# Attention stacks of 64 rows: two heads side by side on the array, 32-row tiles for half of batch 0 only, and a new order of the work

## The reference

```python
x = x + attn(layernorm(x))     # 16 heads of 8, causal, biases on q, k, v and the output
x = x + xattn(layernorm(x), ctx, mask)   # keys and values from 77 context tokens, masked per batch
x = x + ffn(layernorm(x))      # 8 experts of 128x128, gate, top 2 of 8, weights p / sum, halved

scores = einsum('bntd,bnsd->bnts', q, k) / sqrt(D)        # D = 8
scores = where(causal, scores, -inf); attn = softmax(scores); out = einsum(attn, v)
```

## Time and profile before

| | us |
|---|---|
| median of three runs | 424.85 (424.1 to 430.12) |
| the profiled execution | 431.44 |
| its span | 429.6, mean granted clock of TensorE 0.833 |
| TensorE busy | 375.8 (87%) |
| VectorE busy | 255.5 (59%) |
| ScalarE busy | 181.2 (42%) |
| GpSimd busy | 135.1 (31%) |

### The profile page before, as it was taken

How to read it: one execution, slowest core, us unless ns; L and a number is a source line. 1 busy time by engine, 2 the same in 40 slices (tenths; PEclk the granted TensorE clock), 3 DMA queues, 4 the chain that set the end, 5 groups by cost and what they waited for, 6 DMA issues and landing times.

```text
span 429.6 us, 6790 instructions
## 1 busy us (share of the span) xinstructions
PE 375.8 (87%) x2478; PEld 193.3 (45%) x2478; DVE 255.5 (59%) x684; ACT 181.2 (42%) x345; POOL 135.1 (31%) x198
## 2 busy tenths in 40 slices
PE   8989799999987699999789889948789799999593
PEld 3553556344443254445444434315444565724350
DVE  5383645488824499736689988113876324345467
ACT  1712112355675264887560148853445422131100
POOL 3662200122254222125333542221217300005613
PEclk9985555599998699999999989987989855559878
DMA  4654560000036700024320000050000000000000
GB/s 132 147 81 65 92 93 3 1 5 4 1 69 74 83 0 4 7 40 84 58 44 2 5 29 2 2 71 4 2 5 2 24 2 0 2 0 1 27 0 24
DMA packets 19509, 13.82 MB, mean 32 GB/s; under 512 B 2684, under 2 KB 19476, under 8 KB 19476
## 3 DMA queue, kind: packets, MB, share of 16 engines
q1 hardware_dynamic: 19074, 13.04, 17.6%
q10 hardware_dynamic: 402, 0.34, 0.3%
HBM read 2.71 MB, written 1.05 MB: 9 GB/s over the span
## 4 chain that ended last, share of the span: by engine, by line
PE 54%; DVE 23%; ACT 9%; issue 6%; POOL 4%; DMA 3%; ACTq 1%; SPq 1%; DVEq 0%; POOLq 0%
DVE peaks L908 6%; PE banks L1250 6%; PE banks L1061 6%; PE banks L1234 6%; PE banks L1151 5%; PE banks L1053 4%; PE banks L1176 3%; PE banks L1201 3%; PE banks L1275 3%; PE banks L1304 3%; DVE xpeaks L921 3%; PE banks L1266 3%; PE banks L1049 2%; POOL yw L700 2%; PE banks L1082 2%
## 5 line engine op out<-in xcount | busy, mean ns | idle before, releaser
L796 ACT ACTIVATE probs<-banks 128x512 f32<-128x512 f32 x160 | 88.2, 603 | 84.0 <-PE banks L1234 76.0
L908 DVE TENSOR_REDUCE peaks<-banks 128x1 f32<-128x384 f32 (+3 forms) x132 | 76.0, 635 | 24.0 <-PE banks L1176 23.9
L689 POOL TENSOR_SCALAR_AFFINE_SELECT probs<-probs 128x512 f32<-128x512 f32 (+1 forms) x80 | 43.8, 547 | 146.8 <-ACT probs L796 146.8
L1234 PE MATMUL banks<-q_stack,k_stack 102*128 102x512 bf16 (+3 forms) x256 | 55.5, 322 | 3.6 <-ACT probs L796 1.3
L700 POOL TENSOR_TENSOR yw<-yw 128x512 f32<-128x512 f32 (+2 forms) x42 | 34.4, 818 | 63.7 <-issue 32.9
L802 ACT ACTIVATE xprobs<-banks 77x512 f32<-77x512 f32 x64 | 34.3, 604 | 31.6 <-PE banks L1266 24.7
L915 DVE TENSOR_REDUCE peaks<-banks 128x1 f32<-128x128 f32 (+2 forms) x64 | 27.7, 519 | 31.8 <-PE banks L1151 31.8
L1250 PE MATMUL banks<-probs,v_s 128*9 128x256 f32 (+3 forms) x512 | 45.7, 454 | 0.6 <-POOL probs L689 0.3
L1176 PE MATMUL banks<-k_stack,q_stack 96*128 96x512 bf16 (+2 forms) x144 | 44.2, 356 | 0.0
L1167 PE MATMUL banks<-causal,ident_b 128*128 128x128 bf16 (+2 forms) x132 | 33.6, 255 | 7.9 <-issue 6.4
L1234 PEld LDWEIGHTS banks<-q_stack,k_stack 102*128 102x128 bf16 x256 | 20.9, 102 | 42.0 <-issue 17.2
(11 more groups left out here) (168 smaller groups left out, 539.0 us busy)
## 6 DMA issues: line engine op xcount, KB each, us to landing
q_stack<-parts_q SPq DMA_DIRECT2D x24, 128.0 KB, 3.8
k_stack<-parts_k SPq DMA_DIRECT2D x48, 64.0 KB
xq_stack<-parts_x SPq DMA_DIRECT2D x18, 128.0 KB, 4.4
state<-in_x SPq DMA_DIRECT2D x4, 256.0 KB, 4.6
out<-state SPq DMA_DIRECT2D x4, 256.0 KB, 2.3
expert_w_s<-in_expert_w SPq DMA_DIRECT2D x1, 512.0 KB, 4.3
...
```

What stands on the lines that cost most here:

```text
L689: gp.affine_select(out=v, in_=v, compare_op=ALU.is_ge, fill=0.0, base=0, pattern=pattern, channel_multiplier=-1).then_inc(causal_done, 1)
L796: ac.activation(probs[:, grp % 2, u, :], bank_of(step), ACT.Exp, scale=SCALE).then_inc(taken_of(step), 1)
L908: ve.tensor_reduce(dst, bank_of(step)[:, 0:n * width].rearrange("p (h k) -> p h k", h=n), X_AXIS, ALU.max, negate=True).then_inc(taken_of( ...
L1234: last = te.matmul(bank_of(step)[:, col:col + n], k_stack[0:ROWS, b % 2, s, p, 128 * kt:128 * kt + 128], q_stack[0:ROWS, b % 2, p, 128 * k ...
```

## The change

- The stacks have 64 rows for each head (`SLOT`), the two heads of a pair in rows 0 to 63 and 64 to 127. A feature's six parts lie in a step of 8 rows, the mask of the cross attention in row 6 and the maxima, now in two parts, in rows 62 and 63. A product of scores, peaks, cross scores or cross peaks uses 64 rows. `k_stack` and `xk_stack` lose their place for the head.
- The keys are copied by six DMAs of 16 rows, as the queries. Rows that no part fills are cleared: q_stack by ScalarE, xq_stack and xk_stack by GpSimd, k_stack by VectorE.
- The mask is added with 64-row weights (`pick_slot`, `causal_slot`), in two products of 128 columns per head and bank in place of one.
- The peaks of a bank are of heads in the same 64 rows; `SCORES` joins units of the same head slot.
- Only the first half of batch 0 has its peaks in 32-row tiles; the second half uses the stacks. Batch 3's cross attention stays in 32-row tiles.
- The split of the maxima loses its last operation.
- `plan()` has other costs and another `ORDER` and `AHEAD`, and its model of TensorE has tiles, a time for changes of the tiling, and a clock. `WARM` is 0: all products of ones in waits go. Eight at the start (L1066) stay.

The diff, cut to its core:

```diff
-MAX_ROW, ROWS = 96, 102
-MASK_ROW, XMAX_ROW, XROWS = 96, 97, 103
+STEP, SLOT = 8, 64
+MASK_ROW, MAX_ROW, ROWS = 6, 62, 64
 Q_PARTS = (0, 0, 0, 1, 1, 2)
 K_PARTS = (0, 1, 2, 0, 1, 0)
-STACK_DMAS = {"q": len(Q_PARTS), "k": 2 * len(K_PARTS), "x": len(Q_PARTS)}
+STACK_DMAS = len(Q_PARTS)
...
-TILED_PEAKS, TILED_CROSS = 0, B - 1
-
-
-PEAKS = ([(0, [(p, None) for p in (2 * i, 2 * i + 1)]) for i in range(2)]
-         + [(1, [(p, None)]) for p in range(4)]
-         + [(t, [(p, s)]) for t in (2, 3) for p in range(4) for s in range(2)])
+TILED_PEAKS = ((0, 0),)
+TILED_CROSS = B - 1
+
+
+PEAKS = ([(0, s, (0, 1, 2, 3)) for s in range(2)]
+         + [(1, s, (p, p + 1)) for p in (0, 2) for s in range(2)]
+         + [(t, s, (p,)) for t in (2, 3) for p in range(4) for s in range(2)])
 
 TILE_PEAKS = (((0, 0), (1, 128)), ((2, 0),), ((3, 0),))
 
-XPEAKS = [(t, h, n) for t in range(T) for h, n in ((0, 6), (6, 5), (11, 5))]
+XPEAKS = [(s, n, min(n + 6, T * PAIRS)) for n in range(0, T * PAIRS, 6) for s in range(2)]
 
 
 SCORES = ([[(0, j, 0)] for j in range(4)]
           + [[(0, j, 3), (128, j, 1)] for j in range(4)]
-          + [[(0, j, 2), (256, j + 1, 2)] for j in (0, 2)])
+          + [[(0, j, 2), (256, j + 2, 2)] for j in (0, 1)])
...
-BANKS, WARM_BANK = 8, 7
+BANKS, CAUSAL_BANKS = 8, (6, 7)
...
-LATENCY, HOP, SWITCH, RANK, ISSUE = 0.22, 0.05, 0.0, 0.0, 0.62
-AHEAD = {'peak': 4, 'tile_peak': 3, 'xpeak': 2, 'tile_xpeak': 5, 'scores': 2, 'xscores': 5, 'tile_xscores': 5, 'expert': 5}
-
-ORDER = ('scores', 'experts', 'cross', 'scale', 'peaks', 'prepare', 'attend', 'context')
+LATENCY, HOP, SWITCH, ISSUE, LAND = 0.22, 0.05, 0.0, 1.06, 2.7
...
+WARM = 0
+DRAIN, FORCE, CHILL = 0.09, 0, 0
+BIAS = (0.0, 0.0, 0.0, 0.0, 0.0, 0.2, 0.0, 0.0)
+AHEAD = {'peak': 3, 'tile_peak': 3, 'xpeak': 2, 'tile_xpeak': 1, 'scores': 2, 'xscores': 5, 'tile_xscores': 3, 'expert': 6}
+
+ORDER = ('scores', 'cross', 'scale', 'peaks', 'prepare', 'attend', 'context', 'experts')
...
-            key = (start + SWITCH * switch + RANK * rank, rank)
+            key = (start + SWITCH * switch + BIAS[rank], rank)
             if best is None or key < best[0]:
...
-                steps.append(("warm", len(steps), idle))
-            tile = tile_of(step)
+                    steps += [("warm", len(steps), (i, bank_uses[i], count))] * WARM
...
+            size, rows = tile_of(step)
+            if switch:
+                start += DRAIN
+            mode = size
...
         q_stack = sb("q_stack", [128, 2, PAIRS, S], BF16)
-        k_stack = sb("k_stack", [128, 2, 2, PAIRS, S], BF16)
+        k_stack = sb("k_stack", [128, 2, PAIRS, S], BF16)
         xq_stack = sb("xq_stack", [128, PAIRS, S], BF16)
-        xk_stack = sb("xk_stack", [128, 2, PAIRS, B * S2], BF16)
+        xk_stack = sb("xk_stack", [128, PAIRS, B * S2], BF16)
...
-            def copy_queries(n, nth, stack, done):
+            def copy_rows(n, nth, of, stack, cols, done):
 
                 for part, ready in enumerate((high_ready[n], middle_ready[n], low_ready[n])):
                     sp.wait_ge(ready, nth)
-                    for i in range(len(Q_PARTS)):
-                        if Q_PARTS[i] == part:
-                            sp.dma_start(stack[2 * DH * i:2 * DH * i + 2 * DH], parts[n][:, part]).then_inc(done, 16)
-
-            def copy_keys(n, nth, rows, cols, done):
-
-                for part, ready in enumerate((high_ready[n], middle_ready[n], low_ready[n])):
-                    sp.wait_ge(ready, nth)
-                    for i in range(len(K_PARTS)):
-                        if K_PARTS[i] == part:
-                            for s in range(2):
-                                sp.dma_start(rows(2 * DH * i + DH * s, s),
-                                             parts[n][64 * s:64 * s + 64, part, 0:cols]).then_inc(done, 16)
+                    for i in range(len(of)):
+                        if of[i] == part:
+                            sp.dma_start(stack[i:128:STEP], parts[n][:, part, 0:cols]).then_inc(done, 16)
...
-                        wait_cleared(sp, "k_stack")
-                        sp.wait_ge(cleared_by_dve, 1)
+                        sp.wait_ge(cleared_by_dve, 2)
                         for i in range(2):
                             for s in range(2):
-                                r = MAX_ROW + 3 * s
-                                sp.dma_start(k_stack[r:r + 3, i, s], ones).then_inc(ones_stacked, 16)
+                                r = SLOT * s + MAX_ROW
+                                sp.dma_start(k_stack[r:r + 2, i], ones_b[0:2 * PAIRS, :]).then_inc(ones_stacked, 16)
                     stack_free(b)
-                    copy_keys("k", b + 1, lambda r, s: k_stack[r:r + DH, b % 2, s], S, stacked["k"][b % 2])
+                    copy_rows("k", b + 1, K_PARTS, k_stack[:, b % 2], S, stacked["k"][b % 2])
...
+            gp.memset(zeros[:], 0.0).then_inc(cleared, 1)
             gp.memset(ones_b[:], 1.0).then_inc(cleared, 1)
...
+            def clear_queries(i):
+
+                v = q_stack[:, i].rearrange("p a q -> p (a q)").bitcast(F32)
+                ac.copy(v, zeros[:].broadcast_to([128, PAIRS * S // 2])).then_inc(cleared_by_act, 1)
+
+            wait_cleared(act, "zeros")
+            clear_queries(0)
             act.wait_ge(causal_full, 1)
-            ac.copy(causal_rows, banks[:, WARM_BANK].rearrange("p (c k) -> p c k", c=4)).then_inc(causal_ready, 1)
+            ac.copy(causal_rows, banks[:, CAUSAL_BANKS[0]].rearrange("p (c k) -> p c k", c=4)).then_inc(causal_ready, 1)
+            ac.copy(causal_slot[:], banks[:, CAUSAL_BANKS[1], 0:256].rearrange("p (c k) -> p c k", c=2)).then_inc(causal_ready, 1)
...
+                    if kind == "split_k" and b == 0:
+                        clear_queries(1)
...
+            ve.memset(pick_slot[:].bitcast(F32), 0.0)
+            ve.memset(k_stack[:, 0].bitcast(F32), 0.0).then_inc(cleared_by_dve, 1)
...
-                    link(ve.tensor_copy(part[1], left))
-                    ve.tensor_tensor(part[2], left, part[1], ALU.subtract).then_inc(done, 1)
+                    ve.tensor_copy(part[1], left).then_inc(done, 1)
...
-                    t, heads = PEAKS[u]
-                    width = 128 * (t + 1)
+                    t, s, heads = PEAKS[u]
+                    n, width = len(heads), 128 * (t + 1)
                     if u == 0:
-                        pe.wait_ge(stacked["q"][b % 2], 16 * STACK_DMAS["q"] * (b // 2 + 1))
-                        pe.wait_ge(stacked["k"][b % 2], 16 * STACK_DMAS["k"] * (b // 2 + 1))
+                        pe.wait_ge(causal_ready, 2)
+                        pe.wait_ge(pick_slot_ready, 1)
+                        pe.wait_ge(stacked["q"][b % 2], 16 * STACK_DMAS * (b // 2 + 1))
+                        pe.wait_ge(stacked["k"][b % 2], 16 * STACK_DMAS * (b // 2 + 1))
                     bank_free(step)
                     bank = bank_of(step)
-                    n = sum(1 if s is not None else 2 for _, s in heads)
                     diagonal = bank[:, 0:n * width].rearrange("p (h k) -> p h k", h=n)[:, :, width - 128:width]
-                    te.matmul(diagonal, ident_b[:], causal[:, 0:n], start=True, stop=False, skip_group_check=True)
-                    for i, (p, s) in enumerate(heads):
-                        q = q_stack[0:MAX_ROW, b % 2, 4 * f + p, 128 * t:128 * t + 128]
-                        if s is None:
-                            keys = k_stack[0:MAX_ROW, b % 2, :, 4 * f + p, 0:width]
-                            dst = bank[:, 2 * width * i:2 * width * (i + 1)].rearrange("p (s k) -> p s k", s=2)
-                        else:
-                            keys = k_stack[0:MAX_ROW, b % 2, s, 4 * f + p, 0:width]
-                            dst = bank[:, 0:width]
-                        last = te.matmul(dst, q, keys, start=False, stop=(i == len(heads) - 1), skip_group_check=True)
+                    for c in range(2):
+                        te.matmul(diagonal, in_slot(pick_slot, s)[:, 128 * c:128 * c + 128],
+                                  in_slot(causal_slot, s)[:, c].unsqueeze(1).broadcast_to([SLOT, n, 128]),
+                                  start=(c == 0), stop=False, skip_group_check=True)
+                    for i, p in enumerate(heads):
+                        last = te.matmul(bank[:, width * i:width * i + width],
+                                         in_slot(q_stack, s, MAX_ROW)[:, b % 2, 4 * f + p, 128 * t:128 * t + 128],
+                                         in_slot(k_stack, s, MAX_ROW)[:, b % 2, 4 * f + p, 0:width],
+                                         start=False, stop=(i == n - 1), skip_group_check=True)
...
-                        last = te.matmul(bank_of(step)[:, col:col + n], k_stack[0:ROWS, b % 2, s, p, 128 * kt:128 * kt + 128],
-                                         q_stack[0:ROWS, b % 2, p, 128 * kt:S], start=True, stop=True)
```

(2 more changed lines are left out.)

292 lines of the change are left out of this document (173 added, 119 removed).

## The result

The changed kernel takes 377.16 us (median of 4 runs, 375.62 to 379.88) beside 427.49 for the kernel before (median of 4): a ratio of 0.883, interval 0.873 to 0.893.

What follows compares the result with a forecast made beforehand. It took TensorE and VectorE together as the bound, with two TensorE stretches at half clock and gaps between batches. Its eight items summed to -33 us from 431.4, so 398.4, less 6.6 is 392 us; range 364 to 418.

Steps and rivals of the forecast that it cites:

- Items 1 and 2: Start without fourteen products of ones, -1 us (-4 to +2); batch 0's second half in 64-row stacks, -13 us.
- item 2: Batch 0's second half: 64-row products replace 32-row tiles, -11 us, and scores in pairs, -2: -13 (-6 to -20).
- Item 3: Gaps between batches: keys land some 6 us earlier by six DMAs, projections come earlier; 7 us per gap, -14 (-6 to -24).
- item 5: Batch 2's cross stack: TensorE's 8.0 us wait is covered by batch 3's scores and values, -5 us (-8 to 0).
- item 4: 64-row products at full clock, beside batch 0: pairs overlap, against doubled masks and tiling switches, -5 us (-14 to +8).
- no overlap: Rival, 12%: 64-row products don't run together, 32 us of columns return, half beside VectorE: 408 us.
- Item 6: Clock between the long stretches: 10 to 15 us more at 0.50, costing +5 us (0 to +25).
- item 7: Cross attention of batch 3: same products dealt out singly, 13 more switches +1.5, better cover -3: -1 us (-12 to +4).
- item 8: End: without 24 ones in waits, the eight expert products may begin at the lower clock, +1 us, to +3.
- more overlap and a higher clock: Rival, 15%: pairs near full, clock up in much of batch 0 and the last cross attention: about 365 us.
- The clock falls in batches 1 to 3: Rival, 8%: 64-row products there run at 0.50; with 120 us more of it the time is 446 us.
- VectorE and the queues hide it: Rival, 15%: items 3, 4 and 5 give nothing, item 6 costs 8 us: 419 us, no measurable change.

Runs made afterwards that it cites:

- the old layout in the new order: Kernel before (102-row stacks, batch 0 in 32-row tiles, twelve key DMAs, ones in waits) walking the changed kernel's step list: 407.16 us, ratio 0.964 to the kernel before.
- the new layout in the old order: Changed kernel walking the step list of the kernel before, without ones in waits: 424.9 us, ratio 1.006 to the kernel before.
- the run with one half: Changed kernel with every 64-row product reading rows 0 to 63, so no two can run side by side: 414.53 us, ratio 0.973 to the kernel before.
- the heads together: Changed kernel with AHEAD 5 instead of 1 for the last cross attention's tile maxima, so four heads' records stand behind one another: median 374.19 us.
- the tiles are in turn: Changed kernel with the last cross attention's maxima issuing four heads' tiles alternately, one product each, in four banks: 359.12 us, ratio 0.842 to the kernel before.

## Why the prediction was right, and where it was off

Direction, likeliest case and range held: 377.16 lies in 364 to 418 and at the lower edge of the forecast's own 376 to 408. The sum was -33, measured -51.6, and its terms were off in both signs, so that the total came out inside the range is in part luck.

- **Items 1 and 2, start and batch 0** (forecast -14, measured -24.9). The step that failed is that the sum has no term for the first half, which gained 17.4, of it 14.0 by the order alone (36.4 with the old layout). Its 24 tile steps now follow one another without a projection between, and VectorE reduces almost without a gap (10.35 us for 23 maxima from 19.91 on). In the changed kernel the clock is at 1.00 meanwhile, but that is not what the order gives: the old layout in the new order, second line, gets its 14.0 at a mean clock of 0.58. The order of batch 0's first rows was there to be read before, and was not. The second half came to -7.6, within -6 to -20; item 2's -13 was nearer than that looks, since the stacks give 15.7 us in the old order and 11.4 in the new one, where other work had been moved into this stretch (33.1 to 36.9 with the old layout). At the start the ones' loss was rightly feared: the float32 projections at half the clock cost 2 us, and the first tile's mask starts only 0.4 us sooner (15.42 for 15.80).

```profile
19.91 10.35 DVE L978 TENSOR_REDUCE peaks<-banks 128x1 f32<-128x384 f32 x23 [0.51 <-PE banks L1218]
```

```profile
16.00:36.40 20.40, 18.91 (x147) 14.87 (x146) 15.21 (x40) 2.80 (x5) 7.45 (x15) 0.58 0.54 86
```

- **Item 3, stacks and gaps** (forecast -14, measured -17.2 and -25.4). The mechanism was half right: the gaps shrank, to 13.9 and 4.2 us. But I had them bound by the keys' DMAs and capped the gain at 12 us for each. The twelve DMAs cost 2.7 us of the median when put back, within the spread of the executions; the place of the projections in the order did the rest, as the old layout shows with -14.0 and -20.2 in the new order alone. The size to start from was the whole gap (26.7 and 23.1), not the idle at its end.
- **Items 4 to 6, batches 1 to 3** (forecast -5 - 5 + 5, measured +6.9). The cross stack's wait fell from 7.96 us to 0.2 as said in item 5, but its stretch only from 41.1 to 40.1: other work had been moved into it. That is the missing term of all four stretches: with the old layout the new order makes them 13.1 us longer, and the layout then takes 6.2 off, near the -5 of item 4. That line doesn't add up as written (-14 - 6 + 9 is -11; -5 comes out only without the 6), its 86.4 and 104.3, counted over the two lists of steps, go by 0.213 us for 512 columns and not by the 0.22 of its row, and it undersized the pairs: the run with one half is 37 us slower, where the rival "no overlap" has 16. The parts against the pairs (masks twice, switches) are then likely larger too, and no run measured them. Item 6 had the wrong sign for the changed kernel: there is no stretch at 0.50 between 61.7 and 266.5, where there were some 24 us. In the old order its mechanism did show, with some 44 us for 24.

   The Trainium skill (TensorE: Matmul & The Clock Gate, "What's actually happening") says the gate goes by how busy the engine was. Read as time in flight, the windows disagree: with one half TensorE is busy for 32.50 of 32.50 us and stays at 0.50, with pairs it is busy for 21.66 of 24.20 and reaches 0.71.

- **Items 7 and 8, the end** (forecast 0, measured +9.2). One step that failed is item 7's "same products, dealt out singly among others; -1". I read the row of 150 ns each as tiles that do nothing for each other. It is the opposite: alone, a tile's record costs 249 ns (1.99 us for 8), and with the next head behind it 150. Dealt out singly, the 16 heads take 29.1 us instead of 17.9 with the heads together. The same wrong reading stood behind the rival "no overlap". The other step is item 8's +1, up to +3, for the 24 ones that go: with ones back in the waits the end is 5.7 us shorter. The clock goes with both: it is 0.65 in the end as changed and was 0.75 before.

   The Trainium skill (TensorEngine Tiling, Theoretical Speedup) gives up to 4x for 32 rows. The trace agrees where the tiles are in turn: 4 x 1.99 against 2.00 us.

The rivals: "more overlap and a higher clock" was right on batch 0 and the pairs and wrong on the last cross attention, and the time fell between it and the forecast. "The clock falls in batches 1 to 3" did not happen in the changed kernel. "VectorE and the queues hide it" comes near the new layout in the old order in its number alone (419 for 424.9): there batch 0 gave its gain, and the end lost it.

What stays open is why the layout needs the order. By the spans of the table the two alone give 24.7 and 7.1 us and together 51.5, so 19.6 come only of both. Stretch by stretch, what the layout gives in the new order less what it gives in the old one is 9.3 us ahead of batch 3's first split, 5.8 at the end, 2.6 in the first half of batch 0 and 3.3 and 3.5 ahead of the second splits of batches 2 and 3; in the second half of batch 0 it is -4.3. The table shows where, not by which wait.
